# Leaving out TensorE's implied waits in a delta-rule attention pass

## The reference, cut to what matters

```python
x = x + 0.5 * ffn(layernorm(x))     # slot routing: top 8 of 64 slots, GRU on the slots
x = x + attn(layernorm(x))          # gated delta rule, 16 heads of 32
x = x + 0.5 * ffn(layernorm(x))

# attn, for every token t, batch row b and head h:
pred  = state @ k_t
state = a_t * state + b_t * (v_t - pred) outer k_t
out_t = state @ q_t
# then rmsnorm(out) * silu(x Wg), and @ Wo
```

## Time and profile before

| | |
|---|---|
| time, median of 3 runs | 2782.89 us (2769.9 to 2797.73) |
| time of the profiled execution | 2779.95 us |
| its span | 2777.7 us |
| TensorE matmul busy | 2591.8 us, 93% |
| weight loads busy | 1871.6 us, 67% |
| VectorE, GpSimd, ScalarE busy | 67%, 48%, 38% |
| mean granted TensorE clock | 0.972 |

### The profile page before, as it was taken

The page is one execution under the profiler, slowest core; times in us unless marked ns, Lnnn a source line. Parts: engine busy times, 40 slices in busy tenths (PEclk is TensorE's granted clock), DMA queues, the critical chain, the costliest instruction groups (busy, mean ns, idle before and its releaser), DMA issues.

```text
span 2777.7 us, 117151 instructions
## 1 busy us (share of the span) xinstructions
PE 2591.8 (93%) x51052; PEld 1871.6 (67%) x51052; DVE 1857.1 (67%) x5306; ACT 1043.4 (38%) x1962; POOL 1326.3 (48%) x1767
## 2 busy tenths in 40 slices
PE   7999779999999999999999999999999999999768
PEld 6788456666666667766666667776666666776544
DVE  7778456766666767666666677666676667766726
ACT  5777323333333333333333333333333333333220
POOL 2222345554545555555555555555555455555510
PEclk9999999999999999999999999999999999999968
DMA  7342122222222222222222222222222222222178
GB/s 238 104 152 85 24 66 54 62 62 65 65 65 65 64 58 64 57 66 65 57 61 65 65 65 62 65 65 60 54 61 59 65 65 65 65 65 61 54 256 317
DMA packets 365965, 224.78 MB, mean 81 GB/s; under 512 B 277584, under 2 KB 294032, under 8 KB 365456
## 3 DMA queue, kind: packets, MB, share of 16 engines
q1 hardware_dynamic: 356240, 200.51, 25.8%
q10 hardware_dynamic: 9216, 16.78, 1.6%
HBM read 125.49 MB, written 74.97 MB: 72 GB/s over the span
## 4 chain that ended last, share of the span: by engine, by line
PE 84%; DVE 8%; issue 4%; ACT 1%; DMA 1%; POOL 1%; SPq 1%; DVEq 0%; ACTq 0%; POOLq 0%
PE psum L849 24%; PE psum L906 8%; PE psum L1048 8%; PE psum L1029 5%; PE psum L970 5%; PE psum L946 4%; PE psum L1069 4%; PE psum L1009 3%; PE psum L1016 3%; PE psum L690 3%; PE psum L753 3%; PE psum L989 2%; PE psum L836 1%; PE psum L927 1%; PE psum L1089 1%
## 5 line engine op out<-in xcount | busy, mean ns | idle before, releaser
L849 PE MATMUL psum<-w_all,xnT 128*128 128x512 f32 (+2 forms) x2048 | 740.2, 500 | 1.4 <-issue 0.7
L2020 POOL TENSOR_TENSOR sm<-sm,half 128x1 f32<-128x1 f32 (+1 forms) x384 | 530.1, 1381 | 247.0 <-ACT sm L1715 231.0
L849 PEld LDWEIGHTS psum<-w_all,xnT 128*128 128x128 f32 x2048 | 369.0, 191 | 201.8 <-issue 158.2
L2585 DVE TENSOR_TENSOR blk<-blk 128x30 f32<-128x30 f32 (+14 forms) x960 | 327.8, 341 | 33.0
L2583 DVE TENSOR_TENSOR blk<-blk 128x30 f32<-128x30 f32 (+14 forms) x960 | 318.2, 331 | 40.0 <-issue 14.3
L2052 POOL TENSOR_SCALAR sm<-sm 128x1 f32<-128x1 f32 x64 | 14.8, 231 | 625.3 <-DVE sm L2490 625.3
L906 PEld LDWEIGHTS psum<-xnT,w_all 128*128 128x128 f32 x2048 | 256.0, 197 | 42.1 <-issue 34.8
L906 PE MATMUL psum<-xnT,w_all 128*128 128x128 f32 x2048 | 277.2, 285 | 1.5 <-DVE pk L2570 1.5
L1048 PE MATMUL psum<-w_out,gate 128*128 128x512 f32 x512 | 258.4, 618 | 3.0 <-issue 2.0
L1029 PEld LDWEIGHTS psum<-qg,st 32*32 32x32 f32 x8192 | 133.6, 109 | 130.0 <-DVE st L2602 64.7
L2602 DVE STREAM_TRANSPOSE st<-psum 128x128 f32<-128x128 f32 x256 | 81.0, 316 | 189.8 <-PE psum L1029 188.6
(11 more groups left out here) (278 smaller groups left out, 4719.1 us busy)
## 6 DMA issues: line engine op xcount, KB each, us to landing
blk<-n_scratch SPq DMA_DIRECT2D x64, 512.0 KB, 4.4
xin<-in_L_attn_x_dram SPq DMA_DIRECT2D x96, 256.0 KB, 3.1
n_scratch<-nn SPq DMA_DIRECT2D x64, 256.0 KB, 3.4
xh<-xc SPq DMA_DIRECT2D x64, 256.0 KB, 2.3
e_scratch<-blk SPq DMA_DIRECT2D x32, 512.0 KB, 2.8
E<-e_scratch SPq DMA_DIRECT2D x64, 256.0 KB, 3.9
x_scratch<-xh SPq DMA_DIRECT2D x62, 256.0 KB, 2.2
rxn<-in_L_attn_x_dram SPq DMA_DIRECT2D x32, 256.0 KB, 2.9
```

The lines of the kernel that those rows point to most:

```text
L849: last = mm(dst, xnT[b][:, k * P:(k + 1) * P], w_all[:, k * WK + at:k * WK + at + n], start=(k == 0), stop=(k == KC - 1))
L2020: return g.tensor_tensor(dst, a, half[:, 0:n], ALU.pow)
L2585: ins = tt(Y[:, 0:rows, s_ + 1:CH], Y[:, 0:rows, s_ + 1:CH], o, ALU.add)
```

## The change

Waits are taken out of the attention pass's pieces where another wait, of TensorE or of the engines before it, implies them. No matmul, no order, no bank and no other engine's list changes. Counted by the code with the rule above, a full turn has 44 wait-only instructions before and 9 after.

```diff
             def first_xT(n, b):
                 pe.wait_ge(S["xn"], both(n, b))
                 if b == 0:
                     free((n - 1, (T["pt"][1], nth(n - 1, 1))))
-                else:
-                    free((n, (S["x1"], both(n, 1))))
             def proj_k(n, b, part):
                 if part == 0:
-                    pe.wait_ge(S["xnT"], both(n, b))
                     if b == 0:
-                        free((n - 2, (S["ysq"], both(n - 2, 1))), (n - 1, (S["kn"], both(n - 1, 0))))
-                    else:
+                        pe.wait_ge(S["xnT"], both(n, b))
+                    if b == 1:
                         free((n - 1, (T["uw"][0], nth(n - 1, 0))), (n, (S["xnT"], both(n, 1))))
...
             def cum(n):
-                pe.wait_ge(S["la"], n)
                 free((n - 2, (S["slc"], n - 2)), (n - 1, (S["x2"], both(n - 1, 0))), (n, (S["va"], both(n, 0))))
...
             def dec(n, b):
                 pe.wait_ge(S["rhsd"], both(n, b))
-                if b == 0:
-                    free((n - 1, (T["qg"][0], nth(n - 1, 1))))
-                else:
-                    free((n - 1, (T["qg"][0], nth(n - 1, 0))))
...
             def apply_uw(n, b, piece):
                 if piece == 0:
                     pe.wait_ge(e_in[b], 16 * n)
-                    pe.wait_ge(S["va"], both(n, b))
-                    pe.wait_ge(S["vb"], both(n, b))
-                    pe.wait_ge(S["kp"], both(n, b))
-                    if b == 0:
-                        free((n + 1, (S["xnT"], both(n + 1, 1))), (n - 1, (T["qg"][1], nth(n - 1, 1))), (n, (S["kn"], both(n, 1))))
-                    else:
-                        free((n + 1, (T["pt"][0], nth(n + 1, 0))), (n - 1, (S["rxnT"], both(n - 1 + NT, 1))))
...
             def apply_gy(n, b, r):
                 if r == 0:
-                    pe.wait_ge(T["uw"][b], 2 * n)
-                    pe.wait_ge(T["pt"][b], 2 * n)
-                    pe.wait_ge(S["kd"], both(n, b))
                     if b == 0:
-                        free((n, (T["uw"][0], nth(n, 1))))
+                        pe.wait_ge(T["uw"][b], 2 * n)
+                    if b == 0:
+                        pe.wait_ge(S["kd"], both(n, b))
+                    if b == 0:
                         free((n + 1, (S["kn"], both(n + 1, 0))), (n - 1, (S["ysq"], both(n - 1, 1))))
-                    else:
-                        free((n, (S["ysq"], both(n, 0))))
-                        free((n, (S["yv"], both(n, 0))))
```

More of the change, by code:

```diff
@@ L932, in gram @@
                     pe.wait_ge(S["kt"], both(n, b))
-                    pe.wait_ge(S["qt"], both(n, b))
-                    if b == 0:
-                        free((n, (S["qn"], both(n, 0))))
-                    else:
+                    if b == 1:
+                        pe.wait_ge(S["qt"], both(n, b))
+                    if b == 1:
                         free((n, (S["draw"], both(n, 1))))
@@ L940, in gram @@
                         free((n, (S["draw"], both(n, 0))))
-                    else:
-                        free((n, (S["qn"], both(n, 1))))
                 for h in range(piece * NC, (piece + 1) * NC):
@@ L975, in qe_T @@
             def qe_T(n, b, part):
-                pe.wait_ge(S["qe"], both(n, b))
+                if b == 0:
+                    pe.wait_ge(S["qe"], both(n, b))
                 if part == 0:
-                    if b == 0:
-                        free((n, (S["vb"], both(n, 1))))
-                    else:
+                    if b == 1:
                         free((n, (T["uw"][1], nth(n, 0))))
@@ L1034, in y_norm @@
                 pe.wait_ge(S["sqs"], both(n, b))
-                if b == 0:
-                    free((n, (S["ysq"], both(n, 0))))
-                else:
-                    free((n + 1, (S["gate"], both(n + 1, 0))), (n - 1, (S["slc"], n - 1)), (n, (S["x2"], both(n, 0))))
                 mm(ones_at[b], sq[b][:, 0:P], ones[:, 0:1], start=True, stop=True).then_inc(S["ones_ps"], 1)
@@ L1043, in out_proj @@
                     pe.wait_ge(S["y3"], both(n, b))
-                    if b == 0:
-                        free((n + 1, (S["va"], both(n + 1, 0))), (n - 1, (S["hT"], both(n - 1 + NT, 0))), (n, (S["gate"], both(n, 0))))
-                    else:
-                        free((n + 2, (S["x1"], both(n + 2, 0))), (n, (T["qg"][1], nth(n, 0))))
                 last = mm(wo_at[b], gate[b][:, part * P:(part + 1) * P], w_out[:, part * D:(part + 1) * D],
@@ L1054, in last_xT @@
                 pe.wait_ge(S["rxn"], both(n + NT, b))
-                if b == 0:
-                    free((n + 1, (T["pt"][1], nth(n + 1, 0))), (n, (T["qg"][0], nth(n, 0))))
-                else:
-                    free((n, (S["x2"], both(n, 1))))
                 transpose_to(rxT_at[b], rxn[b]).then_inc(S["rxT_ps"], 1)
@@ L1062, in hidden @@
                 if part == 0:
-                    pe.wait_ge(S["rxnT"], both(n + NT, b))
+                    if b == 1:
+                        pe.wait_ge(S["rxnT"], both(n + NT, b))
                     if b == 0:
                         free((n, (S["yv"], both(n, 1))))
-                    else:
-                        free((n + 1, (S["gate"], both(n + 1, 1))), (n, (T["qg"][0], nth(n, 1))))
                 for k in range(KC):
@@ L1075, in logits @@
                 pe.wait_ge(S["hT"], both(n + NT, b))
-                if b == 0:
-                    free((n - 1, (aT, n - 1 + NT)), (n + 2, (S["xnT"], both(n + 2, 0))), (n + 1, (T["pt"][1], nth(n + 1, 1))))
-                else:
-                    free((n, (S["hT"], both(n + NT, 1))))
                 for j2 in range(2):
```

15 lines of the change are left out of this document (1 added, 14 removed).

## The result

| | before | after |
|---|---|---|
| time, median of the runs (us) | 2781.82 (10 runs) | 2759.78 (10 runs) |
| ratio to before, 95% interval | | 0.9905 [0.9884, 0.9926] |
| profiled execution (us) | 2779.95 | 2760.55 |
| span (us) | 2777.7 | 2758.3 |
| mean granted TensorE clock of the span | 0.972 | 0.974 |

The kernel became 22 us faster, 0.95%. The forecast was 2777 us and had 6 us of gain in it. The number lies inside the range of 2740 to 2806 us, which is 66 us wide, but three quarters of the gain are not in the sum.

What follows compares the result with a forecast made beforehand. TensorE's stream plus its idle time was taken to bound the kernel; 2779.95 - 0 - 1.5 - 4 = 2774.5 us for a profiled execution, and with the runs' median 2.9 us higher, 2777 us; range 2740 to 2806 us.

Steps and rivals of the forecast that it cites:

- What bounds the kernel: Whole kernel: TensorE's own stream, busy 93% of the span, plus its idle time; the change can only work on the latter.
- Part 1: Attention pass: 35 fewer wait-only instructions a turn save 0, since queued matmuls cover them.
- The good turn: Attention-pass turn in which all went well: 70.43 us before, forecast at 70.36 us after.
- Rival (a): Attention pass: wait-only instructions do cost TensorE time, thinly spread, worth 76 us, giving 2707 us; chance 8%.
- Part 2: At cum: one wait left, on the load itself, so it starts 0.07 us earlier, 22 times, saving 1.5 us.
- Part 3: Instruction stream: shorter turns shift where 256-instruction blocks begin and TensorE stalls for missing ones; taken as 4 us saved.
- the walk: Block borders in the attention pass move by 26 instructions each turn before, by 9 the other way after.
- The wave: Turn times rising and falling with border position: three ten-turn waves before, one long wave after, crest 75 to 77 us.
- the curve: Turn time as a function of border position, read from the old turns and applied to the new positions.
- Rival (b): At block borders: the sequencer, no longer held, requests the next block earlier; worth 43 us, giving 2740 us; chance 7%.
- Rival (c): Bursts: slow border walk worsens turns as coupling-matrix DMAs meet the block fetch; 2812 us, crest above 80 us; chance 8%.
- The last tile: Behind the pass's last full turn: borders move too, one missing block costing 3.62 us either way as bound; taken as 0.

Runs made afterwards that it cites:

- e2: Changed kernel with nine more wait-only instructions a turn ahead of proj_k, so block borders stand still at a good place; 2713.20 us, ratio 0.9744.
- e3: e2 with 139 wait-only instructions once ahead of first_xT, so block borders stand still at a bad place; 2868.81 us, ratio 1.0298.
- e1: Changed kernel with 35 wait-only instructions a turn put back among the large products, 44 again; 2758.94 us, ratio 0.9903.
- e12: Kernel before with the edits of e5 and e9 together, still 44 wait-only instructions a turn; 2758.79 us, ratio 0.9905.
- e9: Kernel before with three wait-only instructions between gram and apply_uw of row 1 removed, three put ahead of proj_k; 2774.11 us, ratio 0.9964.
- e5: Kernel before with waits exchanged in eleven pieces, the late one onto the weight load, the early one wait-only; 2774.59 us, ratio 0.9967.
- e11: e3 with one wait-only instruction on long-reached values ahead of row 1's apply_uw, behind proj_g's open load; 138 once, not 139; 2894.07 us, ratio 1.0410.
- e7: e3 with one of its nine wait-only instructions a turn now asking for VectorE's late value in row 1's proj_g; 2877.82 us, ratio 1.0337.
- e8: e2 with the last five held wait-only instructions exchanged with the wait on the load; 2715.33 us, ratio 0.9744.

## Why the prediction was right or wrong

**What bounds the kernel** was right: TensorE's own stream, and idle time labelled "issue" at borders 256 instructions apart. e2 and e3, 156 us apart with the same work, leave no doubt. The Trainium skill's page "Advanced Engine Details and Errata", section ISA Cache, gives 128 KB for TensorE and 16 KB, or 256 instructions, for a line. As an estimate from these figures that is eight lines, and with so many ahead e2 and e3 should take the same time; here the measurement decides.

**Part 1**, 35 wait-only instructions at 0, was right. The good turn came out at the 70.36 us that was forecast, and it is 70.37 us in e1 with 44 of them. Rival (a), 2707 us, is out. In the section Network/Comms of the same page the Trainium skill has 50 to 100 ns for reading a semaphore; in the good turn nothing of it is seen, and the one place where such a time shows is `cum`, where 0.12 us became 0.06.

**Part 2**, `cum`, was right: 0.06 us sooner, and the good turn 0.07 shorter. At 20 to 22 such waits that is 1.2 to 1.5 us in all.

**Part 3** was right in the walk and wrong in the size. The wave came about where it was said: it stood at 76.2 us in the 12th turn already, and its crest was over after the 15th, where the curve had it until the 18th. But it was forecast by reading the old turns at new positions, which takes for granted that a border costs the same before and after; the answer was 4 us and the pass gave 20.8. e1 takes the walk back and keeps the gain, so the walk itself is worth nothing that can be measured here (a few us, the 4 among them, can't be told with an interval of 9 us either side), and the curve had changed. One of the two figures behind the 4 us compares unlike things, too: the 2250.5 us were set against the measured 2255.43. Full turns alone as the curve give some 2250 us for the new positions and 2253 for the old, so 3 us less and not 4.9.

**Rival (b)** names what was missing: the sequencer, no longer held, asks for the next block earlier. I gave it 7% on the ground that elsewhere than in `cum` "it is already ahead by a queue full of matmuls". That is the step that failed. Behind the `gram` of row 1 TensorE had work without a break for 4.8 us, and the next block was asked for late all the same: its packet started at 3.07 to 3.29 us, and without the wait-only instructions at 1.04 to 1.12. The rows to read were the first load behind each border, and what VectorE had still to finish then. Its price of 43 us, 60% of the border losses, was twice too high: the stalls in `gram` itself stay (L928, up to 2.4 us), and they stay in e1 and e12 too (6.2 and 5.2 us), so the hold doesn't explain most of them.

That the time fell into the range nevertheless is owed to the range's width, which was laid over the price of rival (b). The sum behind the forecast had the cause of the gain at nothing.

**Rival (c)** had the right meeting of two transfers, the coupling matrices' and the next block's fetch, but as a cost of the change. It was a cost of the kernel before. The crest stayed at 76.8 us and not above 80.

**The last tile** was put at 0. Its turn took 75.37 us before and 76.50 after, inside the bound of one missing block.

The accounting of the 22 us: e9 puts some 10 us [4 to 16] on the three instructions behind the `gram` of row 1, e5 some 9 us [1 to 17] on the exchanged pieces, the 1.5 us of `cum` among them, and e12 has them all. How the 9 us divide among the eleven pieces is open; none was tried alone except `proj_g`. The trace shows less than the 10 us: behind the `gram` stalls of the kernel before `apply_uw` breaks off three times, 0.66 to 0.76 us, 2.1 us together. In two of these three turns the granted clock is at 0.98 besides, which costs some 1.5 us each (below). The rest is not accounted for.

## What to carry to other kernels

Look at what lies between a border of the instruction stream and the request for the next block. In a burst of small products a wait-only instruction, its own value late or standing behind a load that waits, moved the fetch here to the wrong side of another transfer; the same wait on the load itself, with nothing behind it that only waits, didn't. And when a loop's length is a little below a multiple of 256 instructions, a few instructions that do nothing can hold the borders in long products: here 9 in a turn made 2713 us out of 2760, and the wrong place 2869.

## What the runs showed of the hardware

- A wait-only instruction that asks for nothing late is held behind a weight load whose wait is open (e11: the instruction packet 2.89 to 3.37 us behind the border in 28 turns, e3: 1.04 to 1.77), although 35 such instructions elsewhere cost nothing (70.37 us for a good turn with 44 in e1, 70.36 with 9).
- A late instruction packet of 16 KB came behind the data packets: the write of 2,064 small ones begins 1.6 to 1.9 us behind the border, and the packet started behind at least 1,937 of them in all 60 turns of e7, e11 and the kernel before. When it is asked for is not in the trace; that it waited among them, and wasn't asked for later still, is inferred.
- A stall can cost more than its length. In e3 the turn of 1829.45 us has the granted clock at 1.00 and takes 73.37 us; the one of 1004.44, with it at 0.98, takes 74.72, and those at 0.96 up to 77.6. The idle time of the first two is nearly the same (4.31 and 4.13 us); the busy time is 69.06 and 70.59. A mean of 0.98 is a short stay at 1.2 instead of 2.4 GHz. Of the 30 full turns the clock is below 1.00 in 15 before, 9 after, 8 in e12, 5 in e1, 26 in e3, 1 in e2 and none in e8: it goes down in turns with stalls, though not in each (the turn of 2147.61 us before takes 76.81 us at 1.00), and where the stalls go, so does that loss.
